# Dispatch of a mixture of experts: blank rows written behind each expert's last row once the counts are known, and 32 early tiles from twelve batches

## The reference, cut to what matters

```python
logits = (xt @ Wr + br)
probs = softmax(logits); w, idx = top_k(probs, 2); w = w / sum(w)
comb = zeros(T, E).at[arange(T)[:, None], idx].add(w)
h = gelu(einsum('td,edh->teh', xt, W1) + b1)
o = einsum('teh,eho->teo', h, W2) + b2
y = xt + einsum('teo,te->to', o, comb)
```

## Time and profile before

| | us |
|---|---|
| median of three runs | 576.62 |
| lowest and highest run | 572.53, 577.90 |
| the profiled execution, its own time | 575.38 |
| its span (first to last instruction) | 573.6 |
| PE, DVE, ACT, POOL busy in it | 476.2, 398.7, 344.5, 332.8 |

### The profile page before, as it was taken

One profiled execution on the slowest core, in us unless ns is written; L12 is line 12 of the kernel. 1 busy time (PEld: TensorE's weight loads), 2 busy tenths in 40 slices (PEclk: granted clock), 3 DMA queues, 4 the chain that ended last, 5 costly groups with the idle time before them and its releaser, 6 DMA issues. The chain is left out here.

```text
span 573.6 us, 13702 instructions
## 1 busy us (share of the span) xinstructions
PE 476.2 (83%) x4110; PEld 327.3 (57%) x4110; DVE 398.7 (70%) x957; ACT 344.5 (60%) x763; POOL 332.8 (58%) x484
## 2 busy tenths in 40 slices
PE   5777899999999999989886899999768899898700
PEld 4533355555555555554463566666557798787700
DVE  6776778877777777775143799999957895554306
ACT  2026677877777777767722688787745565565400
POOL 3545675565666666513213148888867677777740
PEclk8759999999999999999997999999966999999955
DMA  3675656343444443220009999999954333333239
GB/s 114 139 184 134 178 112 141 95 106 95 104 113 113 113 107 103 81 60 5 2 1 312 381 378 367 365 367 366 359 107 108 89 98 89 94 91 92 65 105 337
DMA packets 78749, 89.93 MB, mean 157 GB/s; under 512 B 8523, under 2 KB 56032, under 8 KB 78688
## 3 DMA queue, kind: packets, MB, share of 16 engines
q1 hardware_dynamic: 72424, 78.82, 46.7%
q0 software_dynamic: 4576, 8.47, 4.4%
q10 hardware_dynamic: 1688, 1.90, 1.4%
HBM read 30.40 MB, written 59.72 MB: 157 GB/s over the span
## 5 line engine op out<-in xcount | busy, mean ns | idle before, releaser
L576 ACT ACTIVATE probs<-p_exp 128x1024 f32<-128x1024 f32 x128 | 131.4, 1027 | 57.9 <-PE p_exp L680 57.4
L450 DVE TENSOR_REDUCE negmax<-p_max 128x4 f32<-128x1024 f32 x103 | 126.0, 1224 | 45.3 <-PE p_max L708 44.6
L1737 POOL DMA_INDIRECT back<-XN2T,rows x79 | 81.5, 1031 | 26.5 <-issue 22.4
L1246 POOL DMA_INDIRECT disp<-pay,pos x64 | 66.2, 1034 | 18.9 <-issue 18.9
L699 PE MATMUL p_out<-probs,V 128*32 128x256 f32 x1024 | 68.3, 385 | 0.0
L680 PE MATMUL p_exp<-QS,KS 64*128 64x256 bf16 x512 | 50.6, 276 | 7.7 <-ACT probs L576 5.3
L1864 ACT ACTIVATE hid<-p_qkv,own 128x128 f32<-128x128 f32 x158 | 45.1, 369 | 18.5 <-PE p_qkv L1885 18.5
L708 PE MATMUL p_max<-KS,QS 61*128 61x256 bf16 x412 | 41.1, 278 | 6.9 <-DMA QS<-scratch 3.9
L1798 DVE TENSOR_SCALAR own<-expert,every_bit 128x578 int32 x79 | 39.1, 537 | 9.5 <-issue 8.4
L680 PEld LDWEIGHTS p_exp<-QS,KS 64*128 64x128 bf16 x512 | 15.0, 94 | 51.3 <-ACT probs L576 30.3
L1885 PE MATMUL p_qkv<-XN2T,own 128*128 128x128 f32 x316 | 43.5, 282 | 0.1
(11 more groups left out here) (274 smaller groups left out, 1158.4 us busy)
## 6 DMA issues: line engine op xcount, KB each, us to landing
disp<-fill SPq DMA_DIRECT2D x8, 4160.0 KB, 38.1
scratch<-part SPq DMA_DIRECT2D x32, 192.0 KB, 2.1
KS<-scratch SPq DMA_DIRECT2D x32, 192.0 KB, 3.4
QS<-scratch SPq DMA_DIRECT2D x28, 192.0 KB, 4.5
rows<-disp SPq DMA_DIRECT2D x79, 65.0 KB, 1.9
scratch<-part SPq DMA_DIRECT2D x32, 128.0 KB, 1.9
own<-back SPq DMA_DIRECT2D x8, 512.0 KB, 8.9
expert<-in_W_dram SPq DMA_DIRECT2D x1, 2064.0 KB, 8.7
```

The costliest lines, as they stand in the source:

```text
L450: dve.tensor_reduce(negmax[q][:, i, :, 2 * hp:2 * hp + 2], bank[:, :].rearrange("p (v w k) -> p v w k", v=HALF, k=S), AX.X, ALU.max, negat ...
L576: act.activation(probs[s % 4][:, :, :, :].rearrange("p v w q -> p (v w q)"), p_exp[:, :], ACT.Exp).then_inc(prob_s.sem, 1)
L1246: pool.indirect_dma_start(out=disp, out_offset=bass.IndirectOffsetOnAxis(ap=pos[q][:, i, k:k + 1], axis=0), in_=pay[q][:, k, i, :], in_off ...
L1737: pool.indirect_dma_start(out=back, out_offset=bass.IndirectOffsetOnAxis(ap=rows[r][:, h, D + 1:ROW].bitcast(U32), axis=0), in_=y[r][:, h, :],
```

## The change

- The nine blank DMAs of the second stage are gone, with their semaphores and POOL's waits for them.
- DVE copies the 16 final counts to whole numbers (`ends`), as the first step of `plan_rest`. SP then writes 128 blank rows behind the last row of each expert (`pad(e)`): it reads the expert's end from `ends` into a register and issues one DMA of 128x130 floats from `fill`. Eight pads stand behind the loads of pair 7, and one behind the loads of each of the pairs 8 to 15. Behind the last one SP waits until all 16 have landed, for the second table and for all scatters, and only then loads pair 16.
- The first table has 32 entries, from the counts of 12 batches, the second 48. The 19 steps of `plan_early` stand at ten sites for each iteration, in n = 16 (2 steps), 17 (10) and 18 (7); the table is turned and packed at n = 19 as before.

```diff
-BLANK = 4
-BLANKS = 3
-N_BLANK = TOKENS // (BLANK * P) + 1
 EARLY_STEPS = 19
-SITES = 8
+SITES = 10
+PLACED = 8
 R3 = 8
-EARLY = 2 * R3
-EARLY_OF = 10
+EARLY = 4 * R3
+EARLY_OF = 12
+EARLY_ENDS = 8
...
-            step = (n - EARLY_OF - 5) * SITES + site
+            step = (n - EARLY_OF - 4) * SITES + site - PLACED
...
                 dve.wait_ge(pos_s.sem, pos_s.at(B - 1, 1))
+                dve.tensor_copy(ends[:, :], counts[0:1, :]).then_inc(ends_s.sem, 1)
                 count_tiles(then, dve, counts, float(P - 1), float(P))
...
-            blanks = disp[0:E * REGION, :].rearrange("(e r) d -> e r d", e=E)
-            for c in range(N_BLANK):
-                n = BLANK if c + 1 < N_BLANK else 1
-                if c >= BLANKS:
-                    sp.wait_ge(blank[c % BLANKS].sem, blank[c % BLANKS].at(c // BLANKS - 1))
-                sp.dma_start(blanks[:, c * BLANK * P:(c * BLANK + n) * P, :].rearrange("e (p n) d -> p e (n d)", n=n),
-                             w["fill"][:, 0:n, :].rearrange("p (o n) d -> p o (n d)", o=1).broadcast_to([P, E, n * ROW]))\
-                    .then_inc(blank[c % BLANKS].sem, 16)
...
-                    if b * S % (BLANK * P) == 0:
-                        c = b * S // (BLANK * P)
-                        pool.wait_ge(blank[c % BLANKS].sem, blank[c % BLANKS].at(c // BLANKS))
...
-                if n == EARLY_OF + 9:
+                if n == EARLY_OF + 7:
                     pack_table(dve, 0, EARLY)
...
-            if isinstance(i, int) and i == R3:
-                sp.wait_ge(table.sem, 2)
...
+            if isinstance(i, int) and i == R3 - 1:
+                sp.wait_ge(w["loaded3"].sem, w["loaded3"].at(0))
+                sp.wait_ge(t["ends_s"].sem, t["ends_s"].at(0))
+                for e in range(EARLY_ENDS):
+                    pad(e)
+            if isinstance(i, int) and R3 <= i < 2 * R3:
+                pad(EARLY_ENDS + i - R3)
+            if isinstance(i, int) and i == 2 * R3 - 1:
+                sp.wait_ge(t["pads"].sem, t["pads"].at(0))
+                sp.wait_ge(table.sem, 2)
+                for q in range(STORED):
+                    sp.wait_ge(t["sent"][q].sem, t["sent"][q].at((B - 1 - q) // STORED))
+
+        def pad(e):
+
+            end = sp.value_load(t["ends"][0:1, e:e + 1], min_val=0, max_val=E * REGION - P)
+            sp.dma_start(disp[bass.ds(end, P), :], w["fill"][:, 0, :]).then_inc(t["pads"].sem, 16)
```

More of the change, by code:

```diff
@@ L1037, in linear_attention_and_routing @@
         table = t["table"]
-        blank = [sig(f"blank{c}", 16) for c in range(BLANKS)]
-        t["blank"] = blank
+        ends, ends_s, pads = tmp("ends", [1, E], I32), sig("ends_s"), sig("pads", 16 * E)
+        t["ends"], t["ends_s"], t["pads"] = ends, ends_s, pads
         fill_set, bsplit = sig("fill_set", 2), sig("bsplit", 6)
@@ L1288, in site @@
             def site(n, s):
-                if 0 <= (n - EARLY_OF - 5) * SITES + s < EARLY_STEPS:
+                if 0 <= (n - EARLY_OF - 4) * SITES + s - PLACED < EARLY_STEPS:
                     early_ready()
@@ L1363, in iteration @@
                         dve.max(best[:, i, :], logits[:, i, :]).then_inc(top_s.sem, 1)
+                site(n, 3)
                 if active(n, 3):
@@ L1376, in iteration @@
                         dve.max_index(where[:, i, :], best[:, i, :], logits[:, i, :]).then_inc(top_s.sem, 1)
-                site(n, 3)
+                site(n, 4)
                 if active(n, 2):
@@ L1389, in iteration @@
                         .then_inc(hot_s.sem, 1)
-                site(n, 4)
+                site(n, 5)
                 if active(n, 5):
@@ L1413, in iteration @@
                     dve.reciprocal(z[:, :], z[:, :]).then_inc(pay_s.sem, 1)
-                site(n, 5)
+                site(n, 6)
                 if active(n, 3):
@@ L1439, in iteration @@
                                       wide(z[:, :].rearrange("p (o i) -> p o i", o=1), [P, TOP, TT]), ALU.mult).then_inc(pos_s.sem, 1)
-                site(n, 6)
+                site(n, 7)
                 if active(n, 3):
@@ L1445, in iteration @@
                     dve.bn_stats(mv[(b + 3) % PAIR][:, TT:2 * TT, :], both_tokens(X, b)).then_inc(st4.sem, 1)
+                site(n, 8)
                 if active(n, 5):
@@ L1456, in iteration @@
                     dve.tensor_scalar(root[n][:, 2, :], mv[n % PAIR][:, :, 2], 1.0 / D, EPS, ALU.mult, ALU.add).then_inc(var_s.sem, 1)
-                site(n, 7)
+                site(n, 9)
             then["bits"](dve)
@@ L1751, in step @@
                     sp.wait_ge(t["sent"][q].sem, t["sent"][q].at((EARLY_OF - 1 - q) // STORED))
-            if isinstance(i, int) and i == R3:
-                sp.wait_ge(table.sem, 2)
             word = sp.value_load(tablei[0:1, 1, bass.ds(2 * i, 1)], min_val=0, max_val=(1 << 2 * PLACE_BITS) - 1)
-            if isinstance(i, int) and i == R3:
-                sp.wait_ge(w["loaded3"].sem, w["loaded3"].at(0))
-                for c in range(N_BLANK - BLANKS, N_BLANK):
-                    sp.wait_ge(t["blank"][c % BLANKS].sem, t["blank"][c % BLANKS].at(c // BLANKS))
-                for q in range(STORED):
-                    sp.wait_ge(t["sent"][q].sem, t["sent"][q].at((B - 1 - q) // STORED))
             if yout[r].due(k - 1):
@@ L1975, in program @@
         w.update(expert=sb("expert", [P, E, EXPERT_ROW]), b_all=sb("b_all", [E, D]),
-                 fill=sb("fill", [P, BLANK, ROW]))
+                 fill=sb("fill", [P, 1, ROW]))
         w["bp"] = w["expert"][:, :, EXPERT:EXPERT_ROW]
```

## The result

The changed kernel takes 581.21 us (median of 12 runs, 577.55 to 587.31), the kernel before 577.28 us beside it (12 runs, 572.53 to 583.66): a ratio of 1.008, with a 95% interval of 1.0048 to 1.0112. It is slower by 0.8%, 4.6 us by the ratio and 3.9 by the medians. The ratio compares fast runs alone and leaves out those more than 1.5% above the fastest of the same kernel (two of each here), which the medians keep. The forecast was 578.2 us against the profiled execution, +2.85 us, within a range of 572.5 to 583.5. The direction was right and the size was not: by the ratio the loss was 1.6 times the forecast.

A forecast was written before the change was run, and what follows sets the result against it. It took POOL and DVE to bound the second stage's loop and POOL the rest to the end. Drain -0.65 us plus pads +3.5 us gave +2.85 us on 575.38, so 578.2 us, range 572.5 to 583.5.

The forecast's parts named there:

- The blanks and the loop: Second stage's loop: removing the blank writes gives 0 there, and the period stays 6.78 us.
- the rival that had the blanks slow the loop: Second stage's loop: without blanks twelve iterations take 6.3 us, not 6.78, giving -5.8 us; chance 0.10.
- The drain: End of the second stage: -1.25 us for ACT's stall plus 0.6 us for planning, -0.65 us in sum.
- ACT's stall for batch 10: End of the second stage: ACT no longer waits for batch 10's last scatter once blanks go, -1.25 us.
- The term of +0.6 us: Iteration 18: PE's table turn waits for the last planning step and delays `p_u`, +0.6 us (bounds 0.3 and 1.0).
- SP's serial time: SP from pair 7 to 16: pads of 1.17 us each delay the loads, so POOL waits for weighted rows.
- +3.5 us: Pads' term: POOL late at pair 14 because pair 16's rows come late, a delay that stays to the end.
- One of the forecast's own signs of being wrong: Among the experts: the forecast is wrong if PEclk shows 0.50 between 455 and 490 us.
- a rival with a chance of 0.06: PE among the experts: its clock falls in the gaps, +7 us over five pairs, 585 us; chance 0.06.
- the pads hide: SP's pads: at 0.95 us a pad POOL never notices them, time 574.7 us; chance 0.25.
- Dearer pads: SP between pairs 7 and 16: at 1.4 us a pad 7.2 us are lost, time 581.9 us; chance 0.17.

The follow-up runs named there:

- the second profile of the changed kernel: The changed kernel unaltered, run again in group B beside the kernel before at 577.51 us: ratio 1.0112, median 583.65 us.
- the kernel that turns the table later: Changed kernel with all pads on ACT, two a step, and PE's first table turn in n = 20 behind `p_u`: 1.0002 of the kernel before.
- the planning alone: Kernel before with only the 32-entry early table from 12 batches and moved planning steps, blanks kept, no pads: 1.0006 in group A, 0.9966 in group B.
- the pads at fixed places: Changed kernel with blank DMAs back and SP's pads written to fixed rows without reading an expert's end: 1.0028 of the kernel before, group C.
- group B: Second group of follow-up kernels, on one chip with the kernel before beside them, which took 577.51 us there.
- the kernel with 11 and 10 matmuls: Changed kernel with 11 and 10 unused PE matmuls added at the ends of steps 7 and 15: 1.0116 of the kernel before, group B.
- group A: First group of follow-up kernels, on one slower chip with the kernel before beside them, which took 623.03 us there.

## Why the prediction was right or wrong

**The blanks and the loop: right.** The period is 6.78 us with and without them; the rival that had the blanks slow the loop has fallen.

**The drain: the size came out by luck, and not for the reasons given.** ACT's stall for batch 10 is gone in the changed kernel: the copy of `ids` at 421.57 us has no wait for a scatter. From power 17 to 18 it is 8.71 us where before had 9.30, -0.59 against the -0.65 of the sum. But the second profile of the changed kernel has 8.99, and from power 14 to 18 it takes 30.67 us where the first has 29.42 and before has 30.00: the same kernel differs from itself by 1.25 us there, twice the effect. (In the second its clock also fell at 404 to 408 us.) The term of +0.6 us inside the sum, PE's table turn ahead of `p_u`, is refuted by the kernel that turns the table later and gains nothing, and the stall of 1.25 us is no fixed price either: the planning alone has all blanks and none of this stall at batch 10 (0.43 us, at another batch). Iteration 18 takes between 8.64 and 9.01 us in all profiles but the first one of before. Which part of the 0.59 is stall and which is PE's clock (0.50 throughout in the changed kernel, back at 1.00 at 425 us before) stays open.

**The surplus of 2.4 us ahead of the loop: not foreseen, and not of the change.** It is whether PE's clock falls between 302 and 307 us. Thirteen profiles have either 5.7 or 8.2 us there: 8.2 in two of before, one of the changed kernel and one of the pads at fixed places, 5.7 in the nine others, with blanks and without. The Trainium skill (TensorE: Matmul & The Clock Gate, The HAM clock gate) warns that the number of slow matmuls varies from run to run of one kernel; here the trace agrees, with 2.5 us between two profiles of the changed kernel at this place. The sum was made against a profile that had the fall; the first profile of the changed kernel had none. So the two profiled spans (573.6 and 575.6) hide part of the loss that the medians show. In all thirteen profiles the 8.2 us come with a fall of the clock and the 5.7 without; what sets a fall off was not tested.

**The pads: that SP's serial time would make the rows late was right, the term was mis-sized.** This is the step that was off: "+3.5 us" for what measured 5.8 (b(0) to b(78), 112.49 - 106.66) in the first pair of profiles, 8.0 (114.57 - 106.59) against the planning alone in group B, and 6.4 in medians when the pads went to ACT. One of the forecast's own signs of being wrong also came: PEclk at 0.50 between 455 and 490 us. Go by the time after b(0) at which POOL takes pair 14:

- Pair 8 was turned 455.58 - 441.18 = 14.4 us after b(0). The forecast's 457.7 + 1.9 - 445.26 is 14.3. Pads of 1.10 and not 1.17 us gave a little back; this step held.
- From there a pair with its pad took 3.13 and not 3.02 us: +0.8 over seven. One issue of a pad was held for 0.58 us.
- The last pad, issued at 476.47, let SP go on at 478.6: 2.1 us, where I took 1.9: +0.2. In the second profile it was 2.7, from 482.83 to 485.5.
- Pair 16 was turned 41.1 us after b(0), with 40.1 forecast, and its predecessor's rows were weighted not 3.0 but 486.33 + 0.42 - 482.25 = 4.5 us later, since PE ran at 0.5 to 0.6: +1.5. This is what I had as a rival with a chance of 0.06, priced by a wrong picture: a clock that stays down for five pairs. In the first profile it fell only behind the two waits, and came back within 4 to 8 us each time.
- POOL's scatter starts 487.57 - 486.75 = 0.82 us after the end of the instruction it waits for. I had 0.1 for that. The number stood in the trace of before:

```profile
448.61 0.41 DVE L1817 TENSOR_TENSOR XN2T<-p_u,rows 128x256 f32<-128x256 f32 x1
```

It ends at 449.02, and POOL's scatter that waited for it starts at 449.84. This is +0.7.

Before that there was a wait that the forecast doesn't have at all, 2.92 us at pair 6. Pair 8's rows were turned when I had said, but pair 6's were weighted 460.21 + 0.42 - 455.58 = 5.05 us later and not 2.96, with PE's clock at 0.50. It doesn't add to the sum at pair 14, where POOL's start is set by pair 16's rows alone.

3.5 + 0.8 + 0.2 + 1.5 + 0.7 is 6.7, and POOL is 46.39 - 39.65 = 6.7 us behind before at pair 14. (Against the planning alone, with 40.63, it is 5.8.) So the terms name places, but their sizes are those of one pair of executions; the clock's 1.5 us are not confirmed by the kernel with 11 and 10 matmuls, whose gain can be anything up to 2 us. By b(78) the delay is 5.8 us. That isn't shown to be catching up: from b(28) to b(78) it is 66.1 us here and 67.0 before, but also 66.0 for the planning alone, which has nothing to catch up, and 67.3 in the second profile of the changed kernel.

**The rivals.** That the pads hide needs 0.95 us a pad; they cost 1.10, and it fell. Dearer pads fell in the first comparison, and came true on the slower chip of group A, with 1.61 us a pad and 1.4% in all. That transfers or the landing are the cause, whoever issues them, which I had not listed, was tested twice and fell as the main cause: on ACT the same transfers cost nothing measurable (1.0002, interval 0.4% to each side), and on SP without the register reads 0.9 of 10.1 us, with two chips compared.

No version beat the kernel before beyond its interval. With the pads on ACT the change is worth nothing (1.0002), which fits blanks that were hidden; the kernel with the pads on ACT and the blanks kept did not run.

## What to carry to other kernels

A queue engine that issues loads just ahead of their use is a resource with a period of its own: count every register read on it, and put new DMAs that need one on an engine that waits anyway. When a wait is new on an engine, add the latency from the end of the awaited instruction to the start of the waiting one (0.82 us here), read from a place where such a wait exists already; and on TensorE look at what its clock did behind waits of that length. And before a difference of two profiles is explained, look at the granted clock stage by stage: the falls that come in some executions of the same kernel are worth as much as the change. Two profiles of one kernel, the second beside the control, show how much that is.

## What the runs showed of the hardware that I had not expected

- On SP a pad of 1.10 us is 0.34 us of issue and, by subtraction, 0.76 us of reading one number into a register and using it. On the slower chips eight pads took 3.73 us without the read and 11.66 with it.
- POOL's back scatter starts 0.82 us after the end of the instruction of DVE that it waited for, in three places (449.02 before; 460.63 and 486.75 changed), and 0.30 us after a scatter of its own.
- PE's clock fell behind waits of 2.77 and 2.47 us, and not in the kernel that filled these waits with matmuls. In the second profile of the changed kernel it fell behind waits of 2.92, 2.26 and 1.84 us.
- The same kernel took 577 us in the first comparison and on the chip of group B, and 623 us on the chips of groups A and C. DVE's sum with `p_u` lasts 425 ns in the median on either, but an iteration of the loop takes 8.5 us and not 6.8 from n = 6 on. In 11 of its 16 batches this sum waits for `p_u`, 13.8 us in all, in the planning-only kernel of group A; in that of group B it waits 4.1 us in 6. One of the 11:

```profile
391.94 0.42 DVE L1422 TENSOR_TENSOR X<-p_u,X 128x256 f32<-128x256 f32 x1 [1.36 <-PE p_u L1566]
```

  What slows these chips was not tested.
